# Graph attention on one core: the low half written over its own logits, four logits buffers, adjacency rows refilled in quarters, and another order at the end of the attention

## The reference

```python
h = relu(layernorm(x))                      # 2048 x 256
ht = (h @ W0).reshape(N, 4, 256)            # four heads
e = leaky_relu(src[:, :, None] + dst[:, None, :], 0.01) + adj[None]
att = softmax(e, axis=-1)                   # per head, 2048 x 2048
x = x + mean over heads of (att @ ht)
h = relu(layernorm(x))
A = (adj != 0);  hidden = h @ W1 + b1
x = x + (A @ hidden) / A.sum(axis=0)[:, None]
```

## Time and profile before

| | us |
|---|---|
| median of 3 runs | 614.52 (614.37 to 615.07) |
| profiled execution, its own time | 613.84 |
| its span in the trace | 611.7 |

### The profile page before, as it was taken

The page is one execution under the profiler, slowest core; times in us unless marked ns, Lnnn a source line. Parts: engine busy times, 40 slices in busy tenths (PEclk is TensorE's granted clock), DMA queues, the critical chain, the costliest instruction groups (busy, mean ns, idle before and its releaser), DMA issues.

```text
span 611.7 us, 9010 instructions
## 1 busy us (share of the span) xinstructions
PE 526.8 (86%) x2991; PEld 301.0 (49%) x2991; DVE 456.6 (75%) x604; ACT 461.3 (75%) x391; POOL 32.8 (5%) x64
## 2 busy tenths in 40 slices
PE   6799669979898798979798898979898999777996
PEld 6333224535454444535444544545455455355885
DVE  5836675978869687869788787879779797263984
ACT  5647775979788788978898888978898895253861
POOL 4000000000000000000000000000000001000211
PEclk9879899999999999989999999999999999888999
DMA  8234151999999999999999999999999999932111
GB/s 330 57 106 183 35 103 33 157 224 216 198 240 206 222 196 219 198 204 211 224 226 209 225 200 226 198 223 206 229 228 209 231 194 203 235 98 91 44 43 43
DMA packets 300319, 108.91 MB, mean 178 GB/s; under 512 B 284748, under 2 KB 295372, under 8 KB 297724
## 3 DMA queue, kind: packets, MB, share of 16 engines
q1 hardware_dynamic: 300296, 108.62, 82.7%
HBM read 30.90 MB, written 6.39 MB: 61 GB/s over the span
## 4 chain that ended last, share of the span: by engine, by line
SPq 41%; PE 17%; ACT 12%; issue 11%; DMA 9%; DVE 9%; DVEq 0%; POOLq 0%; POOL 0%; ACTq 0%
SPq L296 17%; SPq L304 16%; PE ps_relu L804 9%; DMA probs_hi_t<-probs_hi 4%; ACT probs_hi L537 3%; SPq L314 3%; DVE probs_lo L943 3%; ACT logits L529 3%; DMA adj_rows<-in_adj 2%; PE ps_acc L738 2%; DVE logits L934 2%; SPq L266 1%; ACT adj_rows L529 1%; PE ps_acc L714 1%; PE ps_h L714 1%
## 5 line engine op out<-in xcount | busy, mean ns | idle before, releaser
L738 PE MATMUL ps_acc<-h_w_split,probs_hi_t 128*128 128x512 f16 x1024 | 245.4, 384 | 30.8 <-DMA probs_hi_t<-probs_hi 29.1
L521 ACT ACTIVATE ps_relu<-dst_rows,src_bias 128x2048 f32<-128x2048 f32 x64 | 125.9, 1967 | 62.7 <-DVE small L934 62.6
L738 PEld LDWEIGHTS ps_acc<-h_w_split,probs_hi_t 128*128 128x128 f16 x1024 | 93.2, 98 | 147.8 <-DMA probs_hi_t<-probs_hi 36.0
L934 DVE CUSTOM_DVE_ANT_0 logits<-ps_relu,adj_rows 128x2048 f32<-128x2048 f32 x48 | 109.9, 2290 | 52.9 <-DMA adj_rows<-in_adj 44.9
L747 PE MATMUL ps_acc<-h_w_split,probs_lo_t 128*128 128x256 f16 x1024 | 122.3, 273 | 0.3 <-DMA probs_lo_t<-probs_lo 0.3
L943 DVE SCALAR_TENSOR_TENSOR probs_lo<-logits,small,probs_hi 128x2048 f16<-128x2048 f32 x48 | 112.7, 2349 | 7.8 <-ACT probs_hi L537 7.8
L747 PEld LDWEIGHTS ps_acc<-h_w_split,probs_lo_t 128*128 128x128 f16 x1024 | 100.0, 98 | 24.7 <-DMA probs_lo_t<-probs_lo 1.4
L537 ACT ACTIVATE probs_hi<-logits,small 128x2048 f16<-128x2048 f32 x48 | 95.4, 1987 | 0.0
L529 ACT ACTIVATE logits<-logits,small 128x2048 f32<-128x2048 f32 x48 | 95.4, 1987 | 0.0
L804 PE MATMUL ps_relu<-hidden_split,mask_columns 128*128 128x512 f32 x256 | 63.1, 407 | 5.3 <-DVE hidden_split L1032 5.1
L804 PEld LDWEIGHTS ps_relu<-hidden_split,mask_columns 128*128 128x128 f32 x256 | 49.8, 196 | 17.0 <-DVE hidden_split L1032 5.8
(11 more groups left out here) (93 smaller groups left out, 383.7 us busy)
## 6 DMA issues: line engine op xcount, KB each, us to landing
adj_rows<-in_adj SPq DMA_DIRECT2D x16, 1024.0 KB, 5.9
dst_rows<-dst_scratch SPq DMA_DIRECT2D x3, 1024.0 KB, 6.4
x_all<-in_x SPq DMA_DIRECT2D x4, 512.0 KB, 5.7
x<-in_x SPq DMA_DIRECT2D x16, 128.0 KB, 2.5
x_scratch<-x SPq DMA_DIRECT2D x16, 128.0 KB, 1.8
hidden_scratch<-hidden SPq DMA_DIRECT2D x16, 128.0 KB, 2.2
out<-out_rows SPq DMA_DIRECT2D x16, 128.0 KB, 1.7
x_in<-x_scratch SPq DMA_DIRECT2D x1, 1792.0 KB, 8.5
```

What stands on the lines that cost most here:

```text
L521: nc.scalar.activation(R[:, :], D[:, h, :], ACT.Relu, scale=(1.0 - SLOPE) / SLOPE, bias=src[:, bass.ds(u, 1)]).then_inc(relu_ready, 1)
L738: last = nc.tensor.matmul(ACC[parity][:, :], TA[:, e, b, :], H[:, h, b, :], start=(h == 0 and b == 0), stop=False)
L934: nc.vector.tensor_tensor_reduce(out=logits_of(h, parity), in0=R[:, :], in1=ADJ[:, parity, :], scale=-1.0, scalar=3.0e38, op0=ALU.add, op1 ...
```

## The change

1. **Four logits buffers.** E has four heads; head 3 no longer writes over ADJ. `logits_of` is gone.
2. **Low half over its own logits.** PB is gone. `low` writes fp16 over the first half of its own logits row (`low_rows`), and `transpose_lo` reads it there. `low(v)` no longer waits for a transpose; instead `logits(u)` waits until transpose_lo(u - 4) has landed (`lo_in`).
3. **Adjacency by quarters.** `load_adj(ib + 2)` becomes four DMAs of 128 x 512 (256 KB, rows of 2 KB): quarters 0 and 1 in slot (ib, 0), 2 and 3 in slot (ib, 1), around transpose_lo. The first waits for the logits of block ib's head 3 and for mask_rows(ib). Block 1 is still loaded whole, ahead of the slots.
4. **End reordered.** MC lies over E. `load_hidden(0)` moves from slot (15, 0) to (14, 2), `load_hidden(1)` from (15, 2) to (15, 1). `hidden_high(0)` and `hidden_low(0)`, `cast` and `degree` move a slot or two earlier. DVE takes x1_sum(15) and x1_stats(15) ahead of hidden(14), and `degree(2)` behind them. PE transposes h1 of block 14 ahead of the last low matmuls and runs hidden(14) ahead of the first aggregate and hidden(15) after 26 matmuls instead of 42. SP issues the x1 load and the store of x1(15) ahead of the store of hidden(14).

```diff
+        E = place("logits", [P, HEADS, N], fp32)
-        PB = place("probs_lo", [P, 2, N], fp16)
-        MC = alias("mask_columns", [P, BUFS, NB, P], f32r, "probs_hi")
+        MC = [alias(f"mask_columns{j}", [P, NB, P], f32r, "logits", 4 * j * N) for j in range(BUFS)]
...
-            return E[:, h, :] if h < HEADS - 1 else ADJ[:, parity, :]
+        def low_rows(h):
+            return E[:, h, :].bitcast(fp16)[:, 0:N]
...
-            def load_adj(ib, parity):
...
-                    sp.wait_ge(probs_lo_ready, 4 * ib - 4)
...
+            def load_adj(ib, parity, quarter):
+                if quarter == 0:
+                    sp.wait_ge(logits_ready, 4 * ib - 4)
...
+                    sp.wait_ge(mask_rows_ready, ib - 1)
...
+                c = slice(BANK * quarter, BANK * (quarter + 1))
+                sp.dma_start(ADJ[:, parity, c], adj[bass.ds(ib * P, P), c]).then_inc(adj_in[parity], 16)
...
+                ahead = h < 2 and not (isinstance(ib, int) and ib + 2 >= NB)
+                if ahead:
+                    load_adj(ib + 2, parity, 2 * h)
                 if has(u + 2):
-                    transpose_lo(u + 2, h % 2)
-                if h == 2 and not (isinstance(ib, int) and ib + 2 >= NB):
-                    load_adj(ib + 2, parity)
+                    transpose_lo(u + 2, h % 2, (h + 2) % 4)
+                if ahead:
+                    load_adj(ib + 2, parity, 2 * h + 1)
...
+                if isinstance(ib, int) and ib == NB - 2 and h == 2:
+                    sp.wait_ge(logits_ready, UNITS - 4)
+                    load_hidden(0)
+                if final(ib) and h == 1:
+                    sp.wait_ge(logits_ready, UNITS)
                     sp.wait_ge(mask_in, 16 * NB)
-                    load_hidden(0)
-                if final(ib) and h == 2:
-                    sp.wait_ge(probs_lo_ready, UNITS)
                     load_hidden(1)
...
             load_hidden(2)
-            store_hidden(NB - 2)
             sp.wait_ge(unit_multiplied, UNITS - 3)
...
             store_x1(NB - 1)
+            store_hidden(NB - 2)
             store_hidden(NB - 1)
...
+                if final(ib) and h == 3:
+                    transpose_h1(ib - 1)
                 multiply_low(k, h, parity)
...
-                if past(u, HEADS) and h < 3:
-                    vec.wait_ge(probs_lo_ready, u - HEADS + 1)
+                if past(u, HEADS):
+                    vec.wait_ge(lo_in[h % 2], 8 * (u - h % 2) - 16)
...
-                if past(v, 2):
-                    vec.wait_ge(lo_in[h % 2], 16 * k)
...
-            hidden(NB - 2)
-            hidden_low(2)
             x1_sum(NB - 1, 1)
             x1_stats(NB - 1)
+            hidden(NB - 2)
+            degree(2)
+            hidden_low(2)
             norm1(NB - 1)
```

More of the change, by code:

```diff
@@ L600, in _ @@
             hw_high(14)
-            exp(1, 1, 0)
-            high(0, 0, 0, 0)
+            exp(1, 1)
+            high(0, 0, 0)
             for g in range(15, 18):
@@ L606, in _ @@
             hw_high(18)
-            exp(2, 2, 0)
-            high(1, 0, 1, 0)
+            exp(2, 2)
+            high(1, 0, 1)
             for g in range(19, 22):
@@ L773, in slot @@
                     hidden(ib - 2)
+                if final(ib) and h == 3:
+                    transpose_h1(ib - 1)
                 multiply_low(k, h, parity)
-                if h == 3 and past(ib, 1):
+                if h == 3 and past(ib, 1) and not final(ib):
                     transpose_h1(ib - 1)
@@ L1050, in _ @@
             hw_low(16)
-            low(0, 0, 0, 0)
+            low(0, 0)
             row_inverse(1, 1)
@@ L1056, in _ @@
             hw_low(20)
-            low(1, 0, 1, 0)
+            low(1, 1)
             row_inverse(2, 2)
```

99 lines of the change are left out of this document (45 added, 54 removed).

## The result

The changed kernel takes 633.55 us (median of six runs, 630.98 to 635.89), the kernel before 614.44 us in the same session (612.53 to 616.3). The ratio is 1.030, with a 95% interval of 1.027 to 1.033. The forecast was 597 us, its range 584 to 610. The execution that was profiled took 635.89 us and has a span of 633.9 us, against 611.7 before.

A forecast was written before the change was run, and what follows sets the result against it. The prediction took the DMA engines' stream of transfers to bound the loop. From 613.84 us it took 7 for the loop, 3.5 for the first blocks and 7 for the end: 596.3, or 597 against the median; range 584 to 610.

The forecast's parts named there:

- What bounds the loop: Loop: the DMA engines' account of a block sums to 27.2 us against 27.35 measured; the adjacency wait is only a suspect.
- The price of a quarter: Loop: each quarter costs 0.9 us of DMA time, four 3.6 against 4.04 for the whole load; block 26.7 us.
- They cost nothing while that backlog lasts; without it, 1.8 us a block.: Loop, SP's queue: three more issues a block, beside transposes whose issue takes about 2.5 us, counted as free.
- the residual's row: Loop: profile row of the 0.131 MB residual load, costing 0.43 us; doubled to 0.87 us to price a quarter.
- The adjacency's wait: Loop: DVE's 44.9 us in 14 waits for the adjacency would go, but should not be taken for the gain.
- rival 1: Loop: the wait only changes its place, quarters cost 1.01 us, block stays at 27.2; 604 us, chance 0.25.
- DVE's new wait: Loop: logits waits for the low transpose four units back; 0.9 us of margin, counted as nothing.
- First blocks: Start: block 2's adjacency, issued earlier, moves DMA work from the full stretch into an idle one; minus 3.5 us.
- End: From first aggregate to the 192 matmuls: 25.4 us become 17.7; gain 7.7, or 5 if the cover fails; 7 taken.
- Trainium skill's rule: Loop: at least 1 MiB a DMA; three more fixed parts of some 2.0 us, 6 us a block, would give near 680.
- Rival 3: Loop: each quarter leaves a 0.63 us gap and costs 1.5 us, 2.0 us a block more; 630 us, chance 0.12.
- The signs given: Changed profile: no adjacency waits of DVE, loads 26.7 us apart, quarter stretches at 225 GB/s or more, end 17 to 18 us.

The follow-up runs named there:

- e1: The changed kernel with the adjacency as one 1 MB DMA at its old place, in slot 2; 606.4 us, ratio 0.989.
- e2: The changed kernel with the adjacency as one 1 MB DMA ahead of the low transpose of slot 0; 604.2 us, ratio 0.982.
- e7: The changed kernel with ACT and DVE computing only 256 of 2048 columns from unit 4 on, transfers and matmuls in full; 633.7 us, ratio 1.028.
- e8: e2 with ACT and DVE computing only 256 of 2048 columns from unit 4 on; 605.0 us, ratio 0.982.
- g1: The changed kernel with its four quarters issued by ACT's queue in the same slots; 596.7 us, ratio 0.969.
- g4: e2 plus three unused 8 KB loads a block on SP's queue, where the changed kernel has quarters 1 to 3; 629.1 us, ratio 1.023.
- g5: g1 with the loop's two stores and the residual load also on ACT's queue, so SP issues only transposes in a block; 596.1 us, ratio 0.969.
- e12: e2 measured again; 603.8 us, ratio 0.983.
- e3: The changed kernel with its four quarters back to back ahead of the low transpose of slot 0; 614.3 us, ratio 1.000.
- e4: The changed kernel with the adjacency in two 512 KB halves around the first low transpose; 610.5 us, ratio 0.992.
- e6: The changed kernel with each quarter as 32 whole rows of 8 KB, at the same places; 626.8 us, ratio 1.017.
- e11: The changed kernel with the adjacency in two halves, one behind the mask's transpose, one behind the two stores; 611.1 us, ratio 0.993.
- e10: The changed kernel with one whole adjacency load directly behind the mask's transpose, ahead of slot 0's high transpose; 604.1 us, ratio 0.984.
- g6: g1 measured again; 592.2 us, ratio 0.964.
- e5: The kernel before with its adjacency load in slot 2 as four 256 KB DMAs back to back; 622.4 us, ratio 1.013.
- e9: The changed kernel with one whole adjacency load in slot 1, behind the two stores; 606.7 us, ratio 0.987.

## Why the prediction was wrong, point by point

- **What bounds the loop.** Right. The forecast took the wait for the adjacency for a suspect and the stream of transfers for the bound. e1 and e2 show it (50.0 us of waits in the one, none for the adjacency in the other, equal periods), e7 and e8 from the other side.
- **The price of a quarter: here it failed.** The forecast took 0.9 us, near the residual load's row, and so a block of 26.7 us where 29.66 came. By its own account, a whole load costs 4.04 us a block; the changed kernel's period is 2.03 us over e2's, so four quarters cost 6.07, or 1.5 each. That is the upper end that it had worked out (0.87 + 0.63) and put aside because "its start falls on a queue still full of the transpose ahead". g1 shows what was mis-sized: issued from another queue, the four cost 4.04 + 26.9 - 27.6 = 3.3 us by the same account, 0.8 each, so the 0.9 was a fair estimate for the data. The rest comes with the place in SP's queue.
- **"They cost nothing while that backlog lasts; without it, 1.8 us a block."** This is the same step seen from the issue side, and the condition was named and judged wrong. A load between transposes takes the backlog away itself. g4's three tiny loads cost 1.97 us a block with next to no data. The term was in the text with nearly its right size, and was set to zero.
- **Why the residual's row misled.** It was one load in one place, measured by the bytes that passed in 3 us, and the stretch ended at 325, about when the next transpose had been issued (323.00 to 324.54) and before it had landed. In the changed kernel the hollow shows up in the 1.5 to 2 us behind a quarter's issue (143 and 156 GB/s above). Whether the residual load leaves one as well, g5 doesn't show: taking it and the stores away brought nothing.
- **The adjacency's wait.** DVE has none left, as predicted, and the loop got nothing from that: 27.63 and 27.52 us in e2 and e12 against 27.52. That is rival 1, whose 604 us is what e2 and e12 measured (604.2 and 603.8): right about the wait and right for a kernel without quarters; with quarters at its 1.01 us each it would have failed by the same step.
- **DVE's new wait, "counted as nothing".** It appeared, 70.0 us in 36 waits, and it is a symptom. Thinned DVE and ACT leave the time as it is. The forecast had a sign for this: 3 us of such waits a block at a DMA share below 1.0 would mean that latency is the bound. The waits are more than that, the share is 1.00, on the border, and e7 decides against latency.
- **First blocks, -3.5 us.** Wrong in sign for the changed kernel. The first logits of block 2, called for at about 124.5, in the changed kernel:

```profile
129.59 2.29 DVE L940 CUSTOM_DVE_ANT_0 logits<-ps_relu,adj_rows 128x2048 f32<-128x2048 f32 x1 [4.01 <-PE ps_relu L726]
```

  It starts 1.65 us later than in the earlier trace rows and waits for PE, which stands behind a high transpose that took 4.21 us to issue behind the last quarter; PE's eight matmuls there then ran at a granted clock of 0.56, in 3.27 us against 1.90 in e2. With a whole load at the early place the same operation starts at 126.08 (e2) and 126.33 (e12), at the old place at 127.33 (e1). So the move itself is worth 1.0 to 1.3 us, not 3.5, and the quarters take more than that away, by the same term.
- **End, -7 us.** Right: 25.4 us became 18.8, and 17.4 in e2. The last hidden part's cover of 0.4 us held; the one wait left, 1.24 us, is for ACT's mask_columns. It is the term that was read from rows of the same instructions in another order.
- **Against the Trainium skill's rule** (DMA: Bandwidth & Descriptors, Rules for kernel authors, 1 MiB for each DMA). Its direction was right for SP's queue: 0.66 to 0.68 us for each further load at the changed kernel's places. The estimate of 2.0 us for each fixed part (from that page's section on the anatomy of a DMA on the GpSimd path; these DMAs are SP's) was three times too high as a time for which the stream is held. From ACT's queue the rule didn't hold: four DMAs of 256 KB have a shorter period than one of 1 MB, 26.9 against 27.2 us.
- **Rival 3** said 630 us and a point of decision at 1.2 us a quarter. It is what happened; its chance of 0.12 was too low by far. Two of the rows spoke for it (the mask's hollow, the 131 GB/s at the whole load's start), one against it (the residual's stretch), and the forecast followed that one.
- **The signs given.** Quarter stretches below 200 GB/s: 143 to 180. Period over 28: 29.66. Adjacency ends no wait of DVE: so it is. 17 to 18 us behind A: 18.8, with one wait of 1.24 us instead of none over 1.

What stays open: which part of SP's queue's work makes the hollow. The time of the issue alone is hardly it, as four issues in a row (about 2.3 us for the four in e3) cost 0.17 us for each one more; it takes a plain DMA between transposes. Whether that is the start of the next transpose's reads, or the order in which the DMA engines take a queue's work, no run here tells. Nor do they tell why the price of one such load runs from 0.32 us (e4) over 0.49 (e6) and 0.58 (e11 over e10) to 0.66 and 0.68 (g4 and the changed kernel), why g5 gained nothing over g6, or why the profiled execution with GpSimd's queue was worse.

## What to carry to other kernels

When the DMA engines are kept full by one queue, price an added DMA by what its place does to that queue, and not by its bytes: here 8 KB and 256 KB at the same places cost the same 0.66 to 0.68 us, and half a load at one of these places still 0.32. Before a load is cut into pieces, move it to another engine's queue; the same pieces cost 2 us a block on SP's queue and saved 0.7 on ACT's, which made this change 3.1 to 3.6% faster than the kernel before instead of 3% slower. And where a text says "costs nothing while X lasts", work out whether the change itself ends X.

## What the runs showed of the hardware that I had not expected

- Three loads of 8 KB between DMA transposes of the same queue take 0.66 us each from a stream that carries a transpose's 0.524 MB in about 2.45 us (g4; an estimate by 214 GB/s).
- Cut into four in a row, a plain load costs that stream only 0.17 to 0.23 us for each one more (e3, e5).
- The place of a 1 MB load in the stream doesn't matter: 27.63, 27.66, 27.65 and 27.68 us at four places (e2, e9, e10, e1).
- A second queue raised the DMA engines' rate over the loop from 199 to 218 GB/s with the same transfers (g1, between 121 and 475 us).
